# GNN block on Trainium2: row statistics of two slabs by one VectorE instruction

## The reference

```python
def _layernorm(x, axis=-1, eps=1e-05):
    m = jnp.mean(x, axis=axis, keepdims=True)
    v = jnp.var(x, axis=axis, keepdims=True)
    return (x - m) / jnp.sqrt(v + eps)

def reference(x, src, dst, edge_attr_96, W0, b0, g0, be0, W1, b1, g1, be1, mW1, mb1, mW2, mb2):   # names shortened
    h = jnp.maximum(_layernorm(x), 0.0)
    # two graph convolutions, norm = dis[src] * dis[dst], a loop edge on every node
    for W, b, g, be in ((W0, b0, g0, be0), (W1, b1, g1, be1)):
        h = h @ W
        h = jax.ops.segment_sum(h[src] * norm[:, None], dst, num_segments=n) + b
        h = jnp.tanh(h)
        mu = jnp.mean(h, axis=-1, keepdims=True)
        var = jnp.mean(jnp.square(h - mu), axis=-1, keepdims=True)
        h = (h - mu) * jax.lax.rsqrt(var + 1e-5) * g + be
    x = x + h
    h = jnp.maximum(_layernorm(x), 0.0)
    msg = jax.nn.relu(h[src] + edge_attr_96)
    z = h + jax.ops.segment_sum(msg, dst, num_segments=n)
    z = jax.nn.relu(z @ mW1 + mb1) @ mW2 + mb2
    return x + h + jax.nn.relu(z)
```

## Time and profile before

| | |
|---|---|
| median of 3 runs | 2771.33 us (2770.27 to 2777.86) |
| the profiled execution's own time | 2774.01 us |
| its span, first to last instruction | 2772.0 us |
| busy share of the span | DVE 83%, TensorE 76%, ScalarE 73%, GpSimd 58% |
| mean granted TensorE clock | 0.913 of full speed |

### The profile page before, as it was taken

One profiled execution on the slowest core, in us unless ns is written; L12 is line 12 of the kernel. 1 busy time (PEld: TensorE's weight loads), 2 busy tenths in 40 slices (PEclk: granted clock), 3 DMA queues, 4 the chain that ended last, 5 costly groups with the idle time before them and its releaser, 6 DMA issues.

```text
span 2772.0 us, 53972 instructions
## 1 busy us (share of the span) xinstructions
PE 2097.7 (76%) x15433; PEld 1878.9 (68%) x15433; DVE 2290.8 (83%) x8235; ACT 2020.7 (73%) x5708; POOL 1612.2 (58%) x2619
## 2 busy tenths in 40 slices
PE   0210009989999985988888878894399999999988
PEld 0100008988889885877777778784288888887877
DVE  4889857888889865899999999989687887867665
ACT  0029975887889856677777776858499999896856
POOL 5016657777777762777646645440477766755440
PEclk9999999998999977989888887977699999997969
DMA  0049966888889865455555555543466666654542
GB/s 14 2 168 382 371 256 215 278 284 265 280 288 303 293 192 200 140 170 181 179 168 174 171 168 160 179 127 113 125 173 185 173 174 178 175 163 134 148 111 96
DMA packets 262164, 523.50 MB, mean 189 GB/s; under 512 B 101225, under 2 KB 102260, under 8 KB 261864
## 3 DMA queue, kind: packets, MB, share of 16 engines
q1 hardware_dynamic: 217325, 451.15, 47.6%
q0 software_dynamic: 43680, 68.58, 11.4%
q10 hardware_dynamic: 859, 0.23, 0.0%
HBM read 324.98 MB, written 194.81 MB: 188 GB/s over the span
## 4 chain that ended last, share of the span: by engine, by line
PE 42%; DVE 32%; ACT 12%; POOL 6%; issue 4%; DMA 3%; SPq 1%; DVEq 0%; ACTq 0%
PE ps L1250 20%; DVE hot_ L920 7%; ACT rows_f_ L1066 6%; POOL got_f_ L687 6%; PE ps L1285 6%; PE ps L1295 6%; PE ps L1235 5%; DVE stat_b_ L855 5%; DVE stat_a_ L855 5%; PE ps L1266 4%; DVE rows_f_ L993 3%; DVE hot_p_ L749 2%; DVE y_f_ L984 2%; DMA got_f_<-table,src_of 2%; DVE low_f_ L894 2%
## 5 line engine op out<-in xcount | busy, mean ns | idle before, releaser
L687 POOL DMA_INDIRECT got_f_<-table,src_of x1365 | 1453.2, 1065 | 833.3 <-issue 372.8
L1250 PE MATMUL ps<-hot_,high_f_ 128*96 128x304 f32 (+46 forms) x3750 | 1029.1, 309 | 189.9 <-DVE hot_ L920 185.9
L1250 PE MATMUL ps<-hot_,low_f_ 128*96 128x304 f32 (+46 forms) x3750 | 998.4, 304 | 0.0
L1250 PEld LDWEIGHTS ps<-hot_,high_f_ 128*96 128x96 f32 (+1 forms) x3750 | 693.4, 185 | 266.4 <-DVE low_f_ L894 109.8
L920 DVE TENSOR_SCALAR hot_<-node_at,dst_of 128x368 fp32r<-128x368 f32 (+33 forms) x1875 | 792.8, 462 | 42.7 <-PE ps L1250 40.9
L1250 PEld LDWEIGHTS ps<-hot_,low_f_ 128*96 128x96 f32 (+1 forms) x3750 | 695.5, 185 | 30.1
L1079 ACT COPY z_f_<-ps 97x1024 f32<-97x1024 f32 (+2 forms) x294 | 300.5, 1022 | 229.1 <-PE ps L1250 228.4
L1091 ACT ACTIVATE y_f_<-ps,ds 128x96 f32<-128x96 f32 x1568 | 388.0, 374 | 82.5 <-PE ps L1266 81.7
L1235 PE MATMUL ps<-ident_f,in_f_ 128*97 128x128 f32 (+1 forms) x1568 | 219.1, 286 | 267.0 <-DMA in_f_<-table 267.0
L855 DVE BATCH_NORM_STATS2 stat_a_<-y_f_ 128x6 f32<-128x96 f32 x1952 | 383.6, 244 | 2.9 <-ACT y_f_ L1091 2.9
L1235 PEld LDWEIGHTS ps<-ident_f,in_f_ 128*97 128x97 f32 (+1 forms) x1568 | 191.9, 176 | 267.3 <-DMA in_f_<-table 267.3
(11 more groups left out here) (117 smaller groups left out, 2620.0 us busy)
## 6 DMA issues: line engine op xcount, KB each, us to landing
x_f_<-in_x SPq DMA_DIRECT2D x146, 384.0 KB, 4.8
table<-rows_f_ SPq DMA_DIRECT2D x98, 396.0 KB
in_f_<-table SPq DMA_DIRECT2D x98, 396.0 KB
table<-rows_f_ SPq DMA_DIRECT2D x98, 392.0 KB
in_f_<-table SPq DMA_DIRECT2D x98, 392.0 KB
table<-rows_f_ SPq DMA_DIRECT2D x98, 388.0 KB
in_f_<-table SPq DMA_DIRECT2D x98, 388.0 KB
skip<-x_f_ SPq DMA_DIRECT2D x97, 384.0 KB, 3.7
```

The source lines that it names most:

```text
L687: pool.indirect_dma_start(out=got_f[g][:, u * w:(u + 1) * w], out_offset=None, in_=table[:, :], in_offset=bass.IndirectOffsetOnAxis(ap=src ...
L1250: last = pe.matmul(acc[0:w, h, :].rearrange("m (s p) -> m s p", p=P)[:, :, p0:p0 + pw], part[:, u * wide_w:u * wide_w + w], hot_view(slot, ...
```

## The change

`moments` issues one `bn_stats` for two slabs. The instruction reads a view in which the two slabs' elements alternate (element 0 of slab c, element 0 of slab c+1, element 1 of slab c, and so on), so that its even half is one row and its odd half the other; six output numbers are then three for each slab: count, mean, sum of squared deviations. `stat_a` and `stat_b` have 3 numbers for each row in place of 6. The instructions that put halves together (L802 to L816) become one: variance = sum of squares / 96 + eps. The mean is read directly from the statistics tile, where it is every third number. Since that tile is now read later, `moments` waits (`mean_read`) at the first block of a batch for the instruction that read the mean of two batches earlier. `moments` now calls `tick()` 3 times in a block; stage 0 calls it twice more behind each block.

```diff
--- before.py
+++ after.py
@@ -305,11 +305,10 @@
             ds2 = sb("ds2", [P, COLS, 2])
             starts = sb("starts", [1, SUPERS], i32)
             x_f = sbs("x_f", X_RING, [P, S, D])
-            stat_a, stat_b = sbs("stat_a", 2, [P, COLS4, 6]), sbs("stat_b", 2, [P, COLS4, 6])
-            mean_a, scale_a, shift_a, var_a, rstd_a, mean_b, var_c = (
-                sbs(n, 2, [P, COLS4]) for n in ("mean_a", "scale_a", "shift_a", "var_a", "rstd_a", "mean_b", "var_c"))
-            diff_f, sum_f, diff2_f, neg_f, square_f, gap_f = (
-                sb(n, [P, COLS4]) for n in ("diff_f", "sum_f", "diff2_f", "neg_f", "square_f", "gap_f"))
+            stat_a, stat_b = sbs("stat_a", 2, [P, COLS4, 3]), sbs("stat_b", 2, [P, COLS4, 3])
+            scale_a, shift_a, var_a, rstd_a, var_c = (
+                sbs(n, 2, [P, COLS4]) for n in ("scale_a", "shift_a", "var_a", "rstd_a", "var_c"))
+            neg_f, square_f, gap_f = (sb(n, [P, COLS4]) for n in ("neg_f", "square_f", "gap_f"))
             guess_f, power_f = sb("guess_f", [P, COLS4], i32), sbs("power_f", 3, [P, COLS4], i32)
             hot = sbs("hot", HOTS, [P, S * P], f32r)
             got_f = sbs("got_f", QUADS, [P, 4 * (D + 3)])
@@ -796,25 +795,10 @@
                 while waiting:
                     tick()
 
-            def inverse_root(st, at, mean2_t, var_t, to, c):
+            def inverse_root(st, at, var_t, to, c):
 
                 dve.wait_ge(v_step, at)
-                dve.tensor_tensor(diff_f[:, 0:c], st[:, 0:c, 1], st[:, 0:c, 4], ALU.subtract).then_inc(v_step, 1)
-                at = step.up()
-                yield True
-                dve.tensor_tensor(mean2_t[:, 0:c], st[:, 0:c, 1], st[:, 0:c, 4], ALU.add)
-                yield True
-                dve.scalar_tensor_tensor(out=sum_f[:, 0:c], in0=st[:, 0:c, 2], scalar=EPS * D, in1=st[:, 0:c, 5],
-                                         op0=ALU.add, op1=ALU.add)
-                yield True
-                dve.wait_ge(v_step, at)
-                dve.scalar_tensor_tensor(out=diff2_f[:, 0:c], in0=diff_f[:, 0:c], scalar=0.25, in1=diff_f[:, 0:c],
-                                         op0=ALU.mult, op1=ALU.mult).then_inc(v_step, 1)
-                at = step.up()
-                yield True
-                dve.wait_ge(v_step, at)
-                dve.scalar_tensor_tensor(out=var_t[:, 0:c], in0=sum_f[:, 0:c], scalar=1.0 / D,
-                                         in1=diff2_f[:, 0:c], op0=ALU.mult, op1=ALU.add).then_inc(v_step, 1)
+                dve.tensor_scalar(var_t[:, 0:c], st[:, 0:c, 2], 1.0 / D, EPS, ALU.mult, ALU.add).then_inc(v_step, 1)
                 at = step.up()
                 yield True
                 dve.wait_ge(v_step, at)
@@ -850,10 +834,16 @@
                 if stored_before(stage, n):
                     dve.wait_ge(stored[n % 3], stored_before(stage, n))
 
+            mean_read = {}
+
             def moments(st, i, tile):
-                for s in range(S):
-                    last = dve.bn_stats(st[:, i % 4 * S + s, :], tile[:, s, :])
-                    if s < S - 1:
+                if i % 4 == 0 and id(st) in mean_read:
+                    dve.wait_ge(*mean_read[id(st)])
+                for s in range(0, S, 2):
+                    c = i % 4 * S + s
+                    last = dve.bn_stats(st[:, c:c + 2, :].rearrange("p c k -> p (c k)"),
+                                        tile[:, s:s + 2, :].rearrange("p c d -> p d c"))
+                    if s < S - 2:
                         tick()
                 if ends_batch(i):
                     last.then_inc(v_step, 1)
@@ -865,13 +855,14 @@
                 cols = slice(4 * n * S, 4 * n * S + c)
                 if n >= 2:
                     dve.wait_ge(applied, 4 * n - 4)
-                yield from inverse_root(stat_a[j], at, mean_a[j], var_a[j], rstd_a[j][:, 0:c], c)
+                yield from inverse_root(stat_a[j], at, var_a[j], rstd_a[j][:, 0:c], c)
                 dve.tensor_tensor(scale_a[j][:, 0:c], rstd_a[j][:, 0:c], ds2[:, cols, 0], ALU.mult).then_inc(v_step, 1)
                 at = step.up()
                 yield True
                 dve.wait_ge(v_step, at)
-                dve.scalar_tensor_tensor(out=shift_a[j][:, 0:c], in0=mean_a[j][:, 0:c], scalar=-0.5,
+                dve.scalar_tensor_tensor(out=shift_a[j][:, 0:c], in0=stat_a[j][:, 0:c, 1], scalar=-1.0,
                                          in1=scale_a[j][:, 0:c], op0=ALU.mult, op1=ALU.mult).then_inc(scales_done, 1)
+                mean_read[id(stat_a[j])] = scales_done, n + 1
                 yield True
                 batch_free(0, n)
                 dve.tensor_copy(batch_rows(n, D + 1)[:, 0:c, D], ds2[:, cols, 1]).then_inc(cols_done, 1)
@@ -880,6 +871,8 @@
                 k, n = i % len(x0_f), i // 4
                 dve.wait_ge(x0_in[k], 16 * (i // len(x0_f) + 1))
                 at = moments(stat_a[n % 2], i, x0_f[k])
+                tick()
+                tick()
                 if at:
                     waiting.append(small0(n, at))
             rest()
@@ -932,27 +925,30 @@
                         dve.wait_ge(normed_f, 4 * n - 4)
                 else:
                     dve.wait_ge(applied, (layer + 1) * BLOCKS)
-                yield from inverse_root(stat_a[j], at, mean_a[j], var_a[j], rstd_a[j][:, 0:c], c)
+                yield from inverse_root(stat_a[j], at, var_a[j], rstd_a[j][:, 0:c], c)
                 if layer == 1:
-                    dve.scalar_tensor_tensor(out=shift_a[j][:, 0:c], in0=mean_a[j][:, 0:c], scalar=-0.5,
+                    dve.scalar_tensor_tensor(out=shift_a[j][:, 0:c], in0=stat_a[j][:, 0:c, 1], scalar=-1.0,
                                              in1=rstd_a[j][:, 0:c], op0=ALU.mult, op1=ALU.mult).then_inc(scales_done, 1)
+                    mean_read[id(stat_a[j])] = scales_done, 2 * BATCHES + n + 1
                     return
                 dve.tensor_tensor(scale_a[j][:, 0:c], rstd_a[j][:, 0:c], ds2[:, cols, 0], ALU.mult
                                   ).then_inc(scales_done, 1)
                 yield True
                 batch_free(1, n)
                 dve.wait_ge(scales_done, (layer + 1) * BATCHES + n + 1)
-                dve.scalar_tensor_tensor(out=batch_rows(n, D + 3)[:, 0:c, D], in0=mean_a[j][:, 0:c], scalar=0.5,
-                                         in1=scale_a[j][:, 0:c], op0=ALU.mult, op1=ALU.mult)
+                dve.scalar_tensor_tensor(out=batch_rows(n, D + 3)[:, 0:c, D], in0=stat_a[j][:, 0:c, 1], scalar=1.0,
+                                         in1=scale_a[j][:, 0:c], op0=ALU.mult, op1=ALU.mult).then_inc(v_step, 1)
+                mean_read[id(stat_a[j])] = v_step, step.up()
                 yield True
                 dve.tensor_copy(batch_rows(n, D + 3)[:, 0:c, D + 1:D + 3], ds2[:, cols, :]).then_inc(cols_done, 1)
 
             def small2(n, at):
                 c, j = batch_cols(n), n % 2
                 rows_n = batch_rows(n, D + 2)
-                yield from inverse_root(stat_b[j], at, mean_b[j], var_c[j], rows_n[:, 0:c, D + 1], c)
-                dve.scalar_tensor_tensor(out=rows_n[:, 0:c, D], in0=mean_b[j][:, 0:c], scalar=-0.5,
+                yield from inverse_root(stat_b[j], at, var_c[j], rows_n[:, 0:c, D + 1], c)
+                dve.scalar_tensor_tensor(out=rows_n[:, 0:c, D], in0=stat_b[j][:, 0:c, 1], scalar=-1.0,
                                          in1=rows_n[:, 0:c, D + 1], op0=ALU.mult, op1=ALU.mult).then_inc(cols_done, 1)
+                mean_read[id(stat_b[j])] = cols_done, 2 * BATCHES + n + 1
 
             def shift_x(i):
                 k = i % X_RING
```

## The result

The changed kernel takes 2697.5 us (median of 4 runs, 2686.3 to 2699.0) against 2770.8 us of the kernel before in the same comparison: a ratio of 0.973 with a 95% interval of 0.9708 to 0.9752, some 73 us less. The forecast was 2709 us, 62 less, with 2690 to 2730 as its own range.

A forecast was written before the change was run, and what follows sets the result against it. Bounds: ScalarE in stage 0, GpSimd's gathers in layer 0, DVE's instruction list in layer 1, TensorE in layer 2. Gains of 60 + 1.3 + 1 = 62 us gave 2709 us against the median; range 2690 to 2835, own case 2690 to 2730.

The forecast's parts named there:

- The read in turn: New DVE statistics instruction: at 1.035 ns an element plus 61 ns fixed, 260 ns where two took 320.
- Layer 1: DVE's list 66.8 us shorter; 2.8 us lost at the start, and of the 64 left 60 us counted as gain.
- The statistics: Layer 1: 784 pairs, each saving 0.060 us on DVE, 47.0 us together.
- The small ones: Layer 1: small instructions joining halves, five becoming one, save 0.43 us in each of 50 chains, 21.5 us.
- the deduction for TensorE: Layer 1: of 64 us left, 60 counted, since in blocks with many edges TensorE would be the one waited for.
- The 2.8 us at the start: Layer 1: its first 70 us don't run at DVE's speed yet, so 2.8 us of the saving is lost.
- DVE's share of layer 1: Sign of a right forecast: DVE's share of busy time in layer 1 falls below its 97%.
- Stage 0: First batch's shift comes earlier, so ScalarE starts 1.3 us earlier; its work hides DVE's other gain: 1.3 us.
- Layer 0: DVE's list 33 us shorter but covered by GpSimd's gathers; only 1 us gained, behind the last gather.
- layer 0 keeps its length: Sign of a right forecast: layer 0 stays as long as before, with GpSimd still without a gap.
- The bound of 11 us: Layer 0: if the gathers' cover went, a third of DVE's 33 us, 11 us, might show.
- The rivals: Slow read in turn: 2899 us, 0.17; values between: 2834, 0.11; TensorE takes over layer 1: 2740, 0.08; no effect: 0.06.

The follow-up runs named there:

- more_layer0: Changed kernel with two more 192-element statistics instructions per block in layer 0 alone, results unused: layer 0 9 to 11 us longer than the changed kernel.
- four_turn: Changed kernel with each statistics instruction reading four slabs in turn, 48 elements of each: ratio 1.0147 to the kernel before.
- gap24: Changed kernel with each statistics instruction reading its two slabs in steps of 24 bytes, leaving gaps in the streams: ratio 1.0267 to the kernel before.

## Why the prediction was right, and where a term was off

**The read in turn.** Forecast 260 ns, measured 265 to 268 in the blocks shown and 270 as the mean over layer 1. The reason given, that each slab's stream has no gaps and only the turn changes, holds as far as it was tried: by the prediction's estimate of 61 ns of fixed cost an element costs 1.06 to 1.09 ns with two streams, 384 or 1536 bytes apart, near the 1.035 ns of the earlier trace rows, and with gaps in the streams 1.83. It is not the whole rule, since four streams without gaps cost 1.72 to 1.83 as well. The Trainium skill's page "Vector Engine (DVE) Microarchitecture Reference" (5.2 Measured stream behaviour on trn2) agrees on both counts: it has 1.73 ns for a source that hops 4 KiB at every element, and the full rate for a single read stream that alternates between two regions. The rule of the Trainium skill's page "SBUF — State Buffer" (Specifications), by which each crossing to a new line pays, doesn't hold here for two streams: every element crosses, and its price stays within 0.06 ns of that of contiguous elements.

**Layer 1: forecast 60, measured 64 to 68 us** (881.2 and 879.1 against 813.6 and 814.8). The statistics saved a little less than the forecast's 47 us: 53 ns a pair by the unbroken blocks shown, 784 x 0.053 = 42 us; 58 ns by the means over the layer (2 x 164 - 270), 45 us. The small ones saved a little more than 21.5. The prediction read 0.20 us for L802 off, but this is no cost there: the sum's add starts 1.04 us after the gain product with L802 between them (23 blocks) and with nothing between (55 blocks), and still does with L801 (23) or nothing (48) after the change. Since the prediction gave L801 the same 0.20, it drops out. What counts are the other four in a chain of `stat_a`, 0.46 us as a mean over the layer, and in a chain of `stat_b` 0.60 for the five less 0.10 for L801: 25 x (0.46 + 0.50) = 24 us. Reading the mean from every third number cost 0.6 us and not 1.8. The list thus got 65 to 68 us shorter, and the sum said 66.8.

The step that failed is the deduction for TensorE: its 4 us were not lost (DVE waits 8.5 us for it where it waited 9.8). The prediction set TensorE's 634.9 us against a shorter stretch, 86%; in the run it needed 600.65 of 734 us, 82%, at the higher granted clock. Its premise thus didn't come about; whether the 4 us would have been lost at the old clock isn't shown. The 2.8 us at the start agree with the runs: the first gain product starts 68.9 and 69.2 us after the layer's first gather before, 67.1 and 71.0 us after, so up to there nothing is gained that two profiles of one kernel don't differ by. DVE's share of layer 1, which was to fall below its 97%, did not (97.4% before and after): that sign belongs to another engine taking over, and none did. The wait at `mean_read` appears in none of the views as a wait of DVE.

**Stage 0: forecast 1.3, measured 0.8 to 1.2 us.** The shift of the first batch starts 9.1 us after the first statistics (9.5 in the second profile) where it took 10.3 in both profiles before:

```profile
181.06 4.56 DVE L844 BATCH_NORM_STATS2 stat_a_<-x_f_ 128x6 f32<-128x192 f32 x17 [5.20 <-DMA x_f_<-in_x]
...
190.14 0.19 DVE L863 SCALAR_TENSOR_TENSOR shift_a_<-stat_a_,scale_a_ 128x32 f32<-128x32 f32 x1
```

DVE has 31 us less to do there and ScalarE hides it, as forecast: it is busy 208.04 us after 208.06. From the first statistics to the first gather of layer 0 it is 221.2 us in both profiles before, 220.0 and 220.4 after. The table's "until layer 0" doesn't show this, since the first statistics themselves start anywhere from 179.5 to 181.9 us in these four profiles.

**Layer 0: forecast 1, measured 6 to 10 us.** This is the term that was mis-sized. "This is covered by the gathers" took the gathers for a fixed time. They are not. The whole of layer 0 before and after, in the columns of the earlier trace rows:

```profile
403.11:1086.72 683.61, 611.12 (x4852) 578.77 (x4852) 563.64 (x2133) 535.74 (x1793) 490.94 (x456) 0.93 0.79 262
...
401.03:1076.34 675.31, 610.34 (x4852) 582.39 (x4852) 532.21 (x1641) 534.77 (x1793) 483.37 (x455) 0.92 0.80 265
```

With 31 us less on DVE the 455 gathers take 483.4 and 484.1 us for 490.9 and 492.6, and the layer follows one for one. The sign "layer 0 keeps its length" thus failed. The bound of 11 us that was named for a lost cover held, though no cover was lost: for another reason than the one it was made for, so by luck.

Together 66 + 8 + 1 = 75 us, against 73 and 75 in the two comparisons of the medians and the 62 forecast: of the 13 that were missing, some 7 are layer 0's and 6 layer 1's. The rivals fell by their own conditions: the price of an element stayed below 1.48 ns, and TensorE took over nothing.

## What to carry to other kernels

Where short instructions with a fixed cost fill the list of the engine that sets the pace, one that serves two rows saves that cost once; here 53 to 58 ns for each pair of rows that took 320. Price the new access pattern by itself before trusting such a sum: two streams in turn cost almost nothing more, four would have made the kernel 1.5% slower than before the change. And a stage that is covered by another engine's work is only covered as far as that work doesn't itself depend on the engine that is relieved.

## What the runs showed of the hardware that I had not expected

That four streams in turn cost as much as a step of 24 bytes (392 to 412 ns and 412 ns for 192 elements, against 265 for two streams) was open beforehand; three streams weren't tried.

In layer 0 GpSimd's gathers are longer beside some of DVE's work. In the timeline of the changed kernel in layer 0:

```profile
1005.59 0.94 POOL L686 DMA_INDIRECT got_f_<-table,src_of  x1 [0.30 <-PE ps L1246]
1005.73 1.16 DVE L844 BATCH_NORM_STATS2 stat_a_<-y_f_ 128x6 f32<-128x192 f32 x4
1006.80 0.94 DVE L958 TENSOR_TENSOR x_f_<-x_f_,shift_f 128x768 f32<-128x768 f32 x1
1006.84 1.89 POOL L686 DMA_INDIRECT got_f_<-table,src_of  x1 [0.30 <-issue]
1007.66 2.30 DVE L913 TENSOR_SCALAR hot_<-node_at,dst_of 128x304 fp32r<-128x304 f32 x5
```

A gather beside statistics takes 0.94 us, the next, beside an add and the first of five one-hots, 1.89. Sorting the 455 gathers of layer 0 by what DVE does while they run bears this out. In the changed kernel 131 of them run beside this add (mean 1176 ns), 241 beside one-hots and no such add (1040 ns), and the other 83, beside statistics, other instructions or nothing, take 946. From kernel to kernel it is the first group that moves: a mean of 1230 ns in the kernel before, 1228 with `more_layer0`, 1288 with `four_turn` and 1363 with `gap24`, while the second stays at 1025 to 1058 and the third at 946 to 949 in all eleven profiles. So it isn't the statistics that a gather runs beside that stretch it. That the add does is not shown, since one-hots often follow it at once and no run changes either alone; and why more or dearer statistics lengthen the gathers beside the adds stays open.
